# A fused group norm and attention kernel: POOL casts P ahead of the residual sum of the row four behind, DVE takes P's low half first

## The reference

```python
def _L0_conv_ref(x, W_qkv, b_qkv):
    B, G, L, C = x.shape                      # 16, 64, 256, 128
    H = NUM_HEAD                              # 2
    c = C // H
    scale = C ** 0.5
    qkv = jnp.einsum('bglc,dc->bgld', x, W_qkv) + b_qkv
    qkv = qkv.reshape(B, G, L, 3, H, c).transpose(3, 0, 1, 4, 2, 5)
    q, k, v = (qkv[0], qkv[1], qkv[2])
    score = jnp.einsum('bghlc,bghmc->bghlm', q, k) / scale
    score = jax.nn.softmax(score, axis=-1)
    out = jnp.einsum('bghlm,bghmc->bghlc', score, v)
    return out.transpose(0, 1, 3, 2, 4).reshape(B, G, L, C)

x = x + _L0_conv_ref(_gn(x), L0_conv_W_qkv, L0_conv_b_qkv)
```

## Time and profile before

| | |
|---|---|
| median of 3 runs | 4224.27 us (4221.31 to 4226.06) |
| the profiled execution's own time | 4225.53 us |
| its span, first to last instruction | 4223.5 us |
| PE, DVE, ACT, POOL busy, share of the span | 94%, 89%, 74%, 51% |
| mean granted TensorE clock | 0.992 of full speed |
| DMA queues q1 (SP), q10 (ACT), share of 16 engines | 79.7%, 10.7% |

### The profile page before, as it was taken

How to read it: one execution, slowest core, us unless ns; L and a number is a source line. 1 busy time by engine, 2 the same in 40 slices (tenths; PEclk the granted TensorE clock), 3 DMA queues, 4 the chain that set the end, 5 groups by cost and what they waited for, 6 DMA issues and landing times.

```text
span 4223.5 us, 147348 instructions
## 1 busy us (share of the span) xinstructions
PE 3958.7 (94%) x44133; PEld 2923.8 (69%) x44133; DVE 3759.4 (89%) x7138; ACT 3125.2 (74%) x8193; POOL 2134.7 (51%) x3089
## 2 busy tenths in 40 slices
PE   4999999899999999999999899999999999999998
PEld 3767777677776777767777677776767777677776
DVE  6998989889898898988989889898898989989887
ACT  3777777677776777767777677776777777777776
POOL 1555555455554555545555455554555555555554
PEclk9999999999999999999999999999999999999999
DMA  7999898998998989989899998989989998997878
GB/s 197 198 193 201 196 198 196 191 188 199 195 199 181 193 199 198 198 179 200 194 199 198 180 199 197 197 198 181 197 195 201 196 197 193 197 192 166 165 164 167
DMA packets 2438095, 809.81 MB, mean 192 GB/s; under 512 B 2175232, under 2 KB 2437760, under 8 KB 2437760
## 3 DMA queue, kind: packets, MB, share of 16 engines
q1 hardware_dynamic: 2311040, 679.97, 79.7%
q10 hardware_dynamic: 126720, 125.84, 10.7%
HBM read 134.42 MB, written 134.22 MB: 64 GB/s over the span
## 4 chain that ended last, share of the span: by engine, by line
issue 41%; POOL 26%; DVE 15%; POOLq 5%; PE 5%; DVEq 4%; ACT 2%; DMA 1%; SPq 0%; ACTq 0%
POOL p_hi L600 21%; DVE o_norm L455 9%; POOL x_ring L607 4%; POOLq L156 2%; DVEq L460 1%; PE o_bank L315 1%; DVE neg_max L429 1%; POOL y_ring L616 1%; ACT prob L394 1%; PE qk_bank L277 1%; DVE p_lo L436 1%; PE s_bank L299 1%; DVE v_lo L442 1%; POOLq L616 1%; POOLq L607 1%
## 5 line engine op out<-in xcount | busy, mean ns | idle before, releaser
L616 POOL TENSOR_TENSOR y_ring<-image,o_norm 128x256 f32<-128x256 f32 x1024 | 744.5, 727 | 2015.7 <-DVE o_norm L455 2009.9
L394 ACT ACTIVATE prob<-s_bank,neg_max 128x256 f32<-128x256 f32 x4096 | 1604.4, 481 | 189.8 <-issue 177.2
L375 ACT ACTIVATE qk<-qk_bank,b_in 128x256 f32<-128x256 f32 x2048 | 861.0, 472 | 757.2 <-PE qk_bank L277 755.6
L436 DVE SCALAR_TENSOR_TENSOR p_lo<-prob,p_hi 128x1024 f16<-128x1024 f32 x1024 | 1254.3, 1225 | 174.9 <-POOL p_hi L600 144.6
L429 DVE TENSOR_REDUCE neg_max<-s_bank 128x2 f32<-128x512 f32 x2048 | 1309.7, 681 | 35.8 <-PE s_bank L299 35.8
L299 PE MATMUL s_bank<-qk 64*128 64x256 f32 x8192 | 1172.1, 404 | 30.9 <-issue 30.0
L277 PE MATMUL qk_bank<-xc,w_norm 128*128 128x256 f32 x4096 | 1164.2, 407 | 0.0
L600 POOL TENSOR_SCALAR p_hi<-prob 128x1024 f16<-128x1024 f32 x1024 | 1071.4, 1046 | 22.8 <-ACT prob L394 18.1
L277 PEld LDWEIGHTS qk_bank<-xc,w_norm 128*128 128x128 f32 x4096 | 697.1, 190 | 394.9 <-issue 327.0
L299 PEld LDWEIGHTS s_bank<-qk 64*128 64x128 f32 x8192 | 709.4, 187 | 253.2 <-issue 205.3
L315 PE MATMUL o_bank<-v_hi,pt_lo 128*128 128x65 f16 x8192 | 852.9, 193 | 26.6 <-issue 18.0
(11 more groups left out here) (72 smaller groups left out, 2449.4 us busy)
## 6 DMA issues: line engine op xcount, KB each, us to landing
out_dram<-y_ring SPq DMA_DIRECT2D x512, 256.0 KB, 2.5
image<-in_x_dram ACTq DMA_DIRECT2D x240, 512.0 KB, 4.3
pt_hi<-p_hi SPq DMA_TRANSPOSE x1024, 3.3
pt_lo<-p_lo SPq DMA_TRANSPOSE x1024, 3.1
image<-in_x_dram SPq DMA_DIRECT2D x4, 2048.0 KB, 16.2
w_in<-in_L_conv_W_qkv_dram SPq DMA_DIRECT2D x1, 192.0 KB, 2.3
b_in<-in_L_conv_b_qkv_dram SPq DMA_DIRECT2D x3, 0.5 KB, 2.1
```

The costliest lines, as they stand in the source:

```text
L375: ins = act.activation(qk[:, v % 2, t, :], qk_bank[:, t * TOK:(t + 1) * TOK], ACT.Identity, bias=b_in[:, t:t + 1])
L394: ins = act.activation(prob[:, m, c:c + TOK], s_bank[m][h][:, a * TOK:(a + 1) * TOK], ACT.Exp, bias=neg_max[:, m, h, a:a + 1])
L436: dve.scalar_tensor_tensor(out=p_lo[:, v % 2, :], in0=prob[:, v % 2, :], scalar=P_SCALE, in1=p_hi[:, v % 2, :], op0=ALU.mult, op1=ALU.subt ...
L616: pool.tensor_tensor(y_ring[:, m, :], image[:, par, bass.ds(row, 1), :].rearrange("p a c -> p (a c)"), o_norm[:, v % 2, :, :].rearrange("p ...
```

## The change

POOL's order and DVE's order within a step are rewritten. On POOL the cast of row u comes first, then the refill of row u+6, then the residual sum of row u-4. Refill and cast carry leads one higher than before, since they now open a step instead of closing the one before it. On DVE `p_low` goes ahead of `sums`, and `v_low` goes between `sums` and `divide`, with the statistics' places kept in the same sequence between them. No stage and no wait is changed, and PE's, ACT's and SP's orders are the same.

```diff
--- before.py
+++ after.py
@@ -575,13 +575,13 @@
             def order(run, next_image):
+                run(-2, p_low)
                 run(-4, sums)
                 next_image(0)
-                run(-2, p_low)
+                run(-1, v_low)
                 next_image(1)
+                run(-4, divide)
                 next_image(2)
-                run(-4, divide)
-                run(-1, v_low)
                 run(0, row_max, 0)
                 run(0, row_max, 1)
                 next_image(3)
@@ -630,9 +630,9 @@
             def order(run, next_image):
+                run(0, p_high)
+                run(+6, refill)
                 run(-4, finish)
-                run(+5, refill)
-                run(-1, p_high)
```

## The result

The changed kernel takes 4340.86 us (median, 4329.91 to 4369.96) where the kernel before takes 4223.47. The ratio is 1.029, 95% interval 1.027 to 1.032: it is slower by 2.9%. I had forecast 4010.

The account below looks back on a forecast made before the run. Three waiting loops of 3.93 us a row bound the kernel. Gains of 106 (measured rows), 100 (other rows) and 25 (statistics rows), less 15 for late transfers, make 216 off 4223.5: forecast 4010, range 3965 to 4050.

Parts of the forecast that it names:

- The first loop: POOL and DVE: residual sum, cast, p_lo, division, back to residual sum; 3.93 us a row before the change.
- The second loop: PE and DVE: V projection, reciprocal, p_lo, division, v_lo, V projection; 3.93 us before the change, about 2.3 after.
- The paces left behind: What limits next: PE's own work, 3.67 us a row, and DVE's, 3.76 in rows with bn_stats.
- PE is already the bound: Rival, chance 0.1: PE really needs 3.84 us a row, so measured and plain rows stop there; 4080 us.
- the low half moves by 0.3 to 0.7 and the margin falls to about 1.3 on those rows: SP: every second row a store waiting for the residual sum delays transposes; the low half's margin before PE was 2.0 us.
- I add 15 us for late ones: Cost added to the forecast for transposes landing later than the median beside image loads.
- The bound of 150 us for transfers: Upper bound on the cost of late transposes, if every second row waited 0.3 us.
- It turns from a gain into a loss at an overlap of 0.73 us: DVE: per-row overlap of p_lo with POOL's work at which the gain is lost, at 0.52 us for each us.
- the other rule: The skill's rule of full exclusion between p_lo and POOL's SBUF reads; p_lo behind POOL would come some 300 us above 4320.
- the signs of being wrong: p_lo's mean up 0.2 or more; PE waiting for pt_lo or pt_hi in many rows; PE without idle at 3.84.
- p_lo behind POOL: Rival, chance 0.1: the cast starts just ahead of p_lo every row, p_lo takes 0.55 us more; about 4320 us.
- The transfers' rival: Chance 0.14: DMA can't follow below 3.87 us a row, 4080 us; or every second row waits 0.3 us, 4145.

Follow-up runs that it names:

- DVE's part alone: The kernel before with only DVE's order changed to the new one, POOL's order left old; 4592.68 us, ratio 1.088.
- POOL's part alone: The kernel before with only POOL's order changed to the new one, DVE's order left old; 4176.44 us, ratio 0.989.
- the store out of the way: The changed kernel with SP issuing the store in odd steps, for the pair one row older; 4002.18 us, ratio 0.948 to the kernel before.

## Why the prediction was wrong

**The two loops: right.** The first loop is as long as I read it. I gave it 0.44 us more for the division's place in the run with DVE's part alone, and the time came within 0.2% of what this gives. The POOL wait for o_norm went. The second loop I gave as 3.93 with a wait for the cast inside. Without that wait it is 3.76, as an estimate. With POOL's part alone, where this loop stays closed, 20 settled measured rows of image 7 take 77.04 us, 3.85 a row, but DVE is busy all that time, so no run shows this loop as a pace of its own.

**The paces left behind: right.** 3.67 for PE and 3.76 for DVE were what is late next: plain rows run at 3.71 once nothing is held, settled measured rows at 3.72. "PE is already the bound" at 3.84 was wrong. The statistics rows, 4.06 for 4.04, were right too.

**The step that failed: "the low half moves by 0.3 to 0.7 and the margin falls to about 1.3 on those rows", and with it "I add 15 us for late ones".** I named the mechanism, the store on SP behind the late sum, and mis-sized it. In the stall shown the low half is issued 2.8 us late, not 0.7, and 3.3 us before PE wants it. That would still do for the median landing of 3.1, and not for the 5.5 that it took beside a load. The margin that I had at 1.3 us was -2.2. Three things made up the error.

First, I wrote that "the cast comes at least 1 us sooner relative to p_lo" and used that to cancel the delay. The cast ends at 1989.97 and p_lo starts at 1990.00. The exponentials that this cast needs start at 1987.16, in their place in ACT's order and 0.75 us after the maxima that they need have ended. DVE does not hold them up, so in this plain row the cast comes no sooner relative to p_lo than before.

Second, I took the sum at 0.73. It took 1.70. So the high transpose came 2.8 us after the cast's end where I had 1.7, and 0.97 of the 1.1 between them is the shut-out, a term that I cost "at nothing". I had checked whether POOL would hold up p_lo, and found it could not hurt. I had not asked whether p_lo would hold up POOL, and who stood behind that on SP.

Third, I took the median landing for transposes and a lump for loads. The load comes in every fourth row and is no rare event; in image 7's plain rows it costs (75.37 - 60.52)/16 = 0.93 us a row against the same rows of the last image.

**The bound of 150 us for transfers was too small as well.** From 4002 to 4341 it is 339. Part of it is the clock. Three of the four stalls in the first window are followed by a stretch in which the granted clock is at or near half, the lower of its two levels, 1.2 for 2.4 GHz. The fourth, before 1999.98, is not. One of each, five microseconds from the end of the stall on:

```profile
1961.50:1966.50 5.00, 4.95 (x37) 3.63 (x38) 2.86 (x6) 0.47 (x1) 2.07 (x3) 0.50 1.11 235
2000.00:2005.00 5.00, 5.00 (x71) 4.08 (x73) 4.56 (x10) 2.19 (x7) 2.08 (x3) 1.00 1.04 228
```

The first window after the change has 0.91 where the kernel before had 1.00. At half the clock for 18% of 75.37 us, PE does some 7 us less work there than at full clock, of the 16 by which the window exceeds the plain window of the run with the store out of the way, as an upper estimate. Over the whole program the mean granted clock is 0.971 against 0.991 with the store out of the way, which by the same working is at most 90 of the 339 us. No run here tells the clock's part from the waits' own.

**"It turns from a gain into a loss at an overlap of 0.73 us"** rested on 0.5 us for each us of overlap, from one pair of rows. That reading was wrong, as the last section shows. The 300 us that I put on the other rule was also summed wrongly: at 1.05 instead of 0.55 us a row the plain rows, 3.16 + 1.05 = 4.21, are slower by 0.5 as well, some 200 us more over 400 rows.

Of the signs of being wrong that I gave, PE's wait for pt_lo is the one that came. p_lo's mean rose by 0.05, not 0.2, and rows at 3.84 did not come. The 0.12 that I gave to a slower kernel lay almost wholly with p_lo behind POOL, which is not what happened. The transfers' rival (0.14) named the right wait, at 0.3 us a time, and still forecast a gain.

## What to carry to other kernels

When a stage is moved behind another on one engine, follow its result to every in-order queue that waits for it, and then see who stands behind that wait. Here a store with no hurry stood ahead of transposes with a hurry. Ask of two engines that can hinder each other both questions, each one first. And hold a margin against the slowest transfer that comes regularly, not against the median.

## What the runs showed of the hardware

p_lo, with two inputs in SBUF, and POOL's sum and refill, which read SBUF, exclude each other. If p_lo starts first, the sum lasts until p_lo's end and its own time: 1990.28 to 1991.98 is 1.11 us of overlap and 0.73 - 0.14 behind it. If the sum starts first, p_lo takes 1.74 us from 1819.97: 0.66 us of overlap, 1.23, less 0.15. The refill behind that p_lo takes 1.39: 1.13 of overlap, 0.40, less 0.14. The same fixed 0.14 to 0.15 us, and no share, explains the 0.16 that 0.31 us of overlap cost in the earlier trace rows. So the rule of the Trainium skill (SBUF — State Buffer, "Who interferes with whom"), that the second one waits for the whole of the first, holds here but for that 0.15 us, and I was wrong to set the row against it.

The transposes, stores and loads ran at 216 GB/s together in plain rows at 3.71 us, where the same bytes at 3.99 us had looked close to full with a DMA share of 0.98. The share rose to 1.04 there. So a share near 1 was no sign here that the engines could carry no more.
